# Strassen MLP behind a layer of attention on one core: copies, additions and an activation moved ahead of the fill points, two splits regrouped, the bias row by row

## The chip, the cores and the metric

The kernel runs on one NeuronCore of one Trainium2 chip. The metric is the time of one execution on the device in microseconds (us), and lower is better. A core has a matrix engine (PE, TensorE), three engines for elementwise work (DVE is VectorE, ACT is ScalarE, POOL is GpSimd), and SyncE (SP), whose queue in this kernel issues nearly all DMAs. Each engine runs its own instructions strictly in the order in which they are written; engines wait for one another only through semaphores.

## The reference, cut to what matters

The input x has 8 batches of 1024 rows of 512 values. First comes a layer of compressed attention with a residual, then an MLP with a gate and a Walsh-Hadamard transform (fwht) of its hidden values:

```
x = x + attention(layernorm(x), ...)
# attention: c = (x @ W_to_kv.T) @ W_compress.T, layernorm of c, q, k, v of width 64,
# rotary embedding of q and k, causal softmax over 1024 keys, then
# out = z @ W_to_kv + z @ W_out_res.T + b_out_res
x = x + ffn(layernorm(x), W1, W2, W3)
# ffn: hidden = fwht(silu(x @ W1.T) * (x @ W3.T)), 2048 values a row; out = hidden @ W2.T
```

## The kernel before, in words

**Passes and steps.** The MLP is done in 8 passes of 1024 rows, one for each batch, and each pass in 16 steps h = 0 to 15. A step k = 16 s + h (s is the pass) makes one block of 128 hidden features by a Strassen scheme of 7 products, j = 0 to 6, of six matmuls of 128x512 each (lines 1115 to 1117). The products gather in banks of PSUM: ACT copies the first bank out (`copy_b`, L1545) once DVE has finished with it, then a second (`copy_p5`, L1551); DVE adds (`sum_c` L2216, `sum_e` L2220); ACT makes two silus (L1572, `silu(k, 0)` and `silu(k, 1)`), and DVE multiplies each by its partner (`hidden`, L2234). Product 2 of step k+1 writes into the bank that `copy_b` clears, and `copy_b` of step k+1 waits for the last `hidden` of step k.

**The second Strassen.** Every two steps give a pair p of hidden blocks. Out of a pair seven forms are made (A11, S2, S3, A22, A12, S1, S4): sums on POOL (`form_sum`, L2554), and each form is split into a high and a low half-precision part: the high one on ACT (`parts_high`, L1593), the low one, which subtracts the high one, on DVE (`parts_low`, L2240) or on POOL (L2559). `SPLITS` says which forms are split by one instruction. Every four steps give the operands of 14 **units** of 2x6 matmuls of 128x256 (`unit`, lines 1199 to 1201), and one half of a unit follows each of the 7 products of a step. Of the units' results ACT copies some out (`take`, L1601), which POOL then adds to rows of the output (`row_add`, L2572), and DVE adds others itself (`add_unit`, L2249). From step 20 on PE thus alternates: a product, a half unit, a product, a half unit.

**The attention in between.** The attention of the next batch is done in two halves of 512 rows (a is the number of the half), and is spread over the **fill points** of the steps: after product j of step h is fill point f = 7h + j, and in each engine's program `fill(k, j)` issues what is due there. An even a has its slot 0 at f = 3, the odd a behind it 42 points later (`ODD`). The four tiles t of 128 query rows of an a start at the slots `tile_slot(a, t)`: 19, 25, 31 and 37 for an even a, 19, 27, 35 and 43 for an odd one. Names used below: `cproj` (L867, latent projection), `Kl` (L1878), `norm1` (L1928, writes V), `rope_k`/`rope_q` (L1380, L1395), `exps` (L1403 and L1408; it loads the table of the exponential), `low` (L1987, writes Pl, the low part of the softmax), `bias` (L2502, POOL, adds the output's bias to a tile's row of `ring`, four to an a), `tokens_sum`, `tokens_high`, `tokens_low` (L2208, L1538, L2198: the normalized rows for the next pass, by Strassen's forms) and `halves_sum` (L2576, L2259: halves of the rows and weights for W2's forms, made once in passes 0 and 1).

**SP's queue.** `load_forms` (L665) fetches the weights of a step's products (WS), `load_form` (L737) transposes the normalized rows into XF by DMA, `load_form2` (L703) brings W2's forms. `FORMS_AT` says at which j of a step `load_forms` stands.

**What sets the order.** The programs of the engines are written out by hand. Each engine's step function lists its own work between `fill` calls; `take_at(k, j)` and `add_at(k, j)` look up whether a unit's copy or addition is due there. Counters of semaphores (`high_no`, `low_no`) follow that order.

Of the kernel before, what the change touches and what calls it, by code (L numbers as in the profile page):

```python
# [83 lines left out]
TPREP = ({33: 0, 42: 1, 51: 2, 60: 3}, {8: 4, 22: 5, 36: 6, 50: 7})  # L84
# [9 lines left out]
FORMS_AT = {0: 2, 6: 2}  # L94
# [152 lines left out]
def build_kernel(nc, x, xT, w13, w13t, w2, small, cst, tab, wscr, w2scr, w2tmp, w2f, out):  # L247
    with ExitStack() as ctx:
# [335 lines left out]
        def _(sp):  # L584
# [91 lines left out]
            def load_halves(x):  # L676
# [3 lines left out]
                if x in (0, 4):  # L680
                    w.wait_ge(v_xf, xf_no(x // 4, 6))
# [172 lines left out]
        def _(pe):  # L854
# [485 lines left out]
        def _(ac):  # L1340
# [429 lines left out]
            for k in range(NK):  # L1770
# [12 lines left out]
                take_at(k, 0)  # L1783
# [27 lines left out]
                take_at(k, 4)  # L1811
                fill(k, 4)
# [25 lines left out]
        def _(ve):  # L1838
# [186 lines left out]
            def xnorm(a, t):  # L2025
# [3 lines left out]
                if a in (2, 4):  # L2029
                    w.wait_ge(d_tst, 32 * a)  # L2030
# [669 lines left out]
```

## Time and profile before

| | |
|---|---|
| time, median of 3 runs | 2144.19 us (2143.27 to 2144.85) |
| the profiled execution's own time | 2144.14 us |
| its span in the profile | 2142.1 us |
| PE busy | 2010.1 us, 94% |
| DVE, ACT, POOL busy | 1525.1, 1157.8, 1066.0 us |
| granted clock of PE, tenths of full speed, 40 slices | 8 in the first, 9 in the others (9 is 90% or more) |

The profile shows one execution. A row of a timeline gives start, duration, engine, line, operation, tiles, and in brackets how long the engine sat idle before it and what released it. PE's records overlap: a matmul of 128x512 is on record for 0.38 us, but the next one starts 0.22 us behind it. So when a product has to wait, PE loses the idle time in brackets and the overlap of about 0.16 us beside it.

### The profile page before, as it was taken

What the parts mean: (1) busy time and instruction counts of PE and PEld (TensorE: products, weight loads), DVE (VectorE), ACT (ScalarE), POOL (GpSimd) and SP (SyncE); (2) the same over time, 40 slices, a digit from 0 to 9 for tenths busy, and PEclk for the clock granted to TensorE, in tenths of its full rate; (3) what the DMA queues carried; (4) which work ended last, traced back from release to release, by engine and by line L of the source; (5) the groups of instructions that cost most, each with busy time, mean ns of one, the idle gap of its engine ahead of it and who ended that gap; (6) DMA issues with size and microseconds to landing.
All of it is one profiled execution on the core that took longest, in us unless ns stands there. A gap on an engine that the chain in (4) does not pass through costs nothing.

```text
span 2142.1 us, 32782 instructions
## 1 busy us (share of the span) xinstructions
PE 2010.1 (94%) x11862; PEld 1167.0 (54%) x11862; DVE 1525.1 (71%) x2626; ACT 1157.8 (54%) x1775; POOL 1066.0 (50%) x788
## 2 busy tenths in 40 slices
PE   6889899989999999999999999999999999999998
PEld 3534344455555656556555555556565555556665
DVE  7897978758777686776777677776768768653333
ACT  5866455455554655555555646556564555543343
POOL 2356732556356454554546544554644545454444
PEclk8999999999999999999999999999999999999999
DMA  8656346454463524735346434545347353373322
GB/s 328 222 193 228 123 143 164 153 156 138 121 155 125 188 88 142 173 108 164 115 116 171 148 123 123 138 138 163 113 126 178 100 163 113 100 168 125 119 96 89
DMA packets 267264, 312.57 MB, mean 146 GB/s; under 512 B 181344, under 2 KB 191712, under 8 KB 265312
## 3 DMA queue, kind: packets, MB, share of 16 engines
q1 hardware_dynamic: 267104, 310.48, 47.7%
q8 instruction: 95, 1.56, 0.3%
q14 instruction: 65, 0.53, 0.1%
HBM read 221.02 MB, written 47.19 MB: 125 GB/s over the span
## 4 chain that ended last, share of the span: by engine, by line
PE 52%; DVE 19%; ACT 10%; issue 9%; POOL 6%; DMA 3%; SPq 1%; ACTq 0%; DVEq 0%; POOLq 0%
PE PF L1115 10%; PE PF L1117 10%; PE PF L1116 10%; PE PD L1199 4%; PE PD L1200 4%; PE PD L1201 4%; DVE H L2240 2%; POOL ring L2502 2%; DVE XS L2208 2%; DMA WS<-wscr 1%; DVE W2S L2234 1%; DVE Pl L1987 1%; ACT H L1593 1%; PE XY L936 1%; ACT W2S L1572 1%
## 5 line engine op out<-in xcount | busy, mean ns | idle before, releaser
L1115 PE MATMUL PF<-XF,WS 128*128 128x512 f16 x1778 | 676.2, 380 | 25.8 <-ACT PF L1545 10.3
L1116 PE MATMUL PF<-XF,WS 128*128 128x512 f16 x1778 | 674.3, 379 | 0.0
L1117 PE MATMUL PF<-XF,WS 128*128 128x512 f16 x1778 | 674.1, 379 | 0.0
L1199 PE MATMUL PD<-W2S,H 128*128 128x256 f16 x1456 | 397.2, 273 | 33.5 <-ACT W2S L1601 14.8
L1201 PE MATMUL PD<-W2S,H 128*128 128x256 f16 x1456 | 397.1, 273 | 0.0
L1200 PE MATMUL PD<-W2S,H 128*128 128x256 f16 x1456 | 397.1, 273 | 0.0
L2572 POOL TENSOR_TENSOR ring<-ring,W2S 128x512 f32<-128x512 f32 x192 | 257.0, 1341 | 203.2 <-ACT W2S L1601 203.2
L1117 PEld LDWEIGHTS PF<-XF,WS 128*128 128x128 f16 x1778 | 174.0, 98 | 210.1 <-issue 0.7
L1115 PEld LDWEIGHTS PF<-XF,WS 128*128 128x128 f16 x1778 | 173.8, 98 | 193.0 <-issue 36.1
L2554 POOL TENSOR_TENSOR SH<-SH 128x512 f32<-128x512 f32 x112 | 162.2, 1448 | 196.0 <-DVE SH L2234 191.6
L1116 PEld LDWEIGHTS PF<-XF,WS 128*128 128x128 f16 x1778 | 174.3, 98 | 124.2 <-issue 4.8
L1545 ACT ACTIVATE PF<-PF 128x512 f32<-128x512 f32 x127 | 73.9, 582 | 291.2 <-DVE W2S L2234 136.6
L2216 DVE TENSOR_TENSOR PF<-PF,p 128x512 f32<-128x512 f32 x127 | 88.4, 696 | 183.6 <-PE PF L1117 183.6
L1199 PEld LDWEIGHTS PD<-W2S,H 128*128 128x128 f16 x1456 | 142.4, 98 | 132.5 <-issue 30.2
L1572 ACT ACTIVATE SH<-PF,afs 128x512 f32<-128x512 f32 x144 | 98.9, 687 | 206.4 <-PE PF L1117 113.2
L1200 PEld LDWEIGHTS PD<-W2S,H 128*128 128x128 f16 x1456 | 142.5, 98 | 81.3
L2554 POOL TENSOR_TENSOR W2S<-W2S,SH 128x512 f32<-128x512 f32 x56 | 75.2, 1343 | 214.7 <-DVE H L2240 214.7
L1601 ACT ACTIVATE W2S<-PD,afs 128x512 f32<-128x512 f32 x224 | 152.6, 681 | 9.8 <-PE PD L1201 8.5
L1201 PEld LDWEIGHTS PD<-W2S,H 128*128 128x128 f16 x1456 | 142.5, 98 | 16.6
L2234 DVE SCALAR_TENSOR_TENSOR SH<-PF,afs,SH 128x512 f32<-128x512 f32 x144 | 107.4, 747 | 57.8 <-ACT SH L1572 48.6
L1572 ACT ACTIVATE W2S<-PF,afs 128x512 f32<-128x512 f32 x112 | 77.0, 688 | 118.3 <-PE PF L1117 117.9
L2220 DVE TENSOR_TENSOR PF<-PF,p 128x512 f32<-128x512 f32 x127 | 87.7, 691 | 69.7 <-PE PF L1117 69.3
(371 smaller groups left out, 3606.0 us busy)
## 6 DMA issues: line engine op xcount, KB each, us to landing
WS<-wscr SPq DMA_DIRECT2D x112, 896.0 KB, 4.9
W2S<-w2f SPq DMA_DIRECT2D x196, 256.0 KB, 2.7
ring<-x SPq DMA_DIRECT2D x56, 256.0 KB, 5.3
wscr<-WS SPq DMA_DIRECT2D x16, 896.0 KB, 4.2
out<-ring SPq DMA_DIRECT2D x56, 256.0 KB, 3.2
RAW<-w13t SPq DMA_DIRECT2D x16, 512.0 KB, 4.6
xraw<-xT SPq DMA_DIRECT2D x28, 256.0 KB, 4.1
XF<-w SPq DMA_DIRECT2D x13, 512.0 KB, 18.1
```

What stands on the lines that cost most here:

```text
L1115: pe.matmul(bank, wh, th, start=i < 2 and j == 0, stop=False, skip_group_check=True)
L1116: pe.matmul(bank, wh, tl, start=False, stop=False, skip_group_check=True)
L1117: m = pe.matmul(bank, wl, th, start=False, stop=j == 1, skip_group_check=True)
L1199: pe.matmul(o, th, wh, start=i in (P1, P2, P5) and tp == 0 and r == 0, stop=False, skip_group_check=True)
L1200: pe.matmul(o, th, wl, start=False, stop=False, skip_group_check=True)
L1201: m = pe.matmul(o, tl, wh, start=False, stop=r == 1, skip_group_check=True)
L1572: ac.activation(sh(k)[:, i, :], PF[:, (1 - k % 2, 2)[i], :], ACT.Silu, scale=afs[:, k % NH:k % NH + 1]).then_inc((a_sb, a_sc2)[i], 1)
L1601: ac.activation(TT[:, u % 2, :], PD[:, u % 2, :], ACT.Copy, scale=afs[:, 65:66]).then_inc(a_T, 1)
L2216: ve.tensor_tensor(PF[:, 2, :], PF[:, k % 2, :], p5[:, :], ALU.add).then_inc(v_c, 1)
L2234: ve.scalar_tensor_tensor(o, PF[:, (k % 2, 3)[i], :], afs[:, 16 + h:17 + h], o, ALU.mult, ALU.mult).then_inc((v_hA, v_hE)[i], 1)
L2554: gp.tensor_tensor(o, a, b, op).then_inc(g_S, 1)
L2572: gp.tensor_tensor(r, r, TT[:, g, :].rearrange("p (t c) -> p t c", t=2), ALU.add).then_inc(g_r, 1)
```

## The change

- **Splits regrouped.** A12 is split by itself as soon as it is there (ACT behind `copy_b`, DVE ahead of `sum_c`); so S4 can be summed on POOL at j = 2 instead of j = 3, and S4 and A22 are split together by one instruction of 1024 columns: ACT at the end of the even step, POOL at j = 0 of the odd step. Before, A12 and A22 were one split of 1024 columns on ACT and DVE, and S4 one of 512 on ACT and POOL.
- **Copies and additions of units** stand ahead of the fill point at which they stood behind it (`take_at`, `add_at`), and `silu(k, 1)` of steps above 16 stands ahead of fill point 4. DVE's `hidden(k, 1)` stands behind fill point 5 where that one holds a `low`.
- **Bias row by row.** POOL's four additions of an attention's bias were two calls of two rows at slots 12 and 13; now each row has its own call, four slots behind its tile's start.
- **W2's halves** (`TPREP`) are prepared later: two in pass 0 and six in pass 1, where there were four and four.
- **Smaller ones.** At h = 0 `load_forms` stands at j = 1 instead of 2 on SP; `cproj` of k 0 and 1 at slot 3 instead of 2 for a from 3 on; the drain at the end is reordered.

```diff
-PLACE_A = {"A11": (0, 0), "S3": (1, 8), "S1": (2, 3), "S2": (4, 4), "A12": (5, 6), "A22": (7, 7), "S4": (16, 17)}
-SPLITS = (("A11", "S3"), ("S1", "S2"), ("A12", "A22"), ("S4",))
+PLACE_A = {"A11": (0, 0), "S3": (1, 8), "S1": (2, 3), "S2": (4, 4), "A12": (16, 17), "A22": (7, 7), "S4": (5, 6)}
+SPLITS = (("A11", "S3"), ("S1", "S2"), ("A12",), ("S4", "A22"))
-TPREP = ({33: 0, 42: 1, 51: 2, 60: 3}, {8: 4, 22: 5, 36: 6, 50: 7})
+TPREP = ({48: 0, 59: 1}, {8: 2, 18: 3, 28: 4, 38: 5, 48: 6, 58: 7})
-FORMS_AT = {0: 2, 6: 2}
+FORMS_AT = {0: 1, 6: 2}
+def low_at(k, j):
+    s, h = divmod(k, NH)
+    return s > 0 and any(slot == tile_slot(c, t) + 2 for c, slot in slots(s, 7 * h + j) for t in range(4))
 # PE
-                if slot in (2, 5):
-                    for k in (0, 1) if slot == 2 else (2, 3):
+                if slot in (2 if a < PLAIN else 3, 5):
+                    for k in (2, 3) if slot == 5 else (0, 1):
 # ACT, one step
+                if k > 4 * QF + 1 and k % 2 == 0:
+                    parts_high(k // 2 - 1, 2)
-                take_at(k, 0)
+                take_at(k, 1)
                 fill(k, 0)
                 if k:
                     copy_p5(k)
-                if k > 4 * QF + 2 and k % 2:
-                    parts_high((k - 3) // 2, 3)
-                take_at(k, 1)
+                take_at(k, 2)
                 fill(k, 1)
...
-                take_at(k, 4)
-                fill(k, 4)
+                take_at(k, 5)
+                if k <= 4 * QF:
+                    fill(k, 4)
                 silu(k, 1)
-                take_at(k, 5)
+                if k > 4 * QF:
+                    fill(k, 4)
+                take_at(k, 6)
                 fill(k, 5)
+                if k > 4 * QF + 1 and k % 2 == 0:
+                    parts_high(k // 2 - 1, 3)
-                take_at(k, 6)
 # DVE, one step
                     hidden(k - 1, 0)
+                    add_at(k, 0)
                     fill(k - 1, 6)
...
+                if k > 4 * QF + 1 and k % 2 == 0:
+                    parts_low(k // 2 - 1, 2)
-                add_at(k, 1)
+                add_at(k, 2)
                 fill(k, 1)
                     sum_c(k)
...
-                add_at(k, 5)
+                if low_at(k, 5):
+                    fill(k, 5)
                 hidden(k, 1)
-                fill(k, 5)
                 add_at(k, 6)
+                if not low_at(k, 5):
+                    fill(k, 5)
 # POOL
                     if j == 0:
+                        if k > 4 * QF + 2:
+                            parts_low((k - 3) // 2, 3)
                         form_sum(k // 2, 0)
-                    if j == 1 and k > 4 * QF + 2:
-                        parts_low((k - 3) // 2, 3)
-                    if j == 3:
+                    if j == 2:
                         form_sum(k // 2 - 1, 3)
-                if slot in (12, 13):
-                    w.wait_ge(v_V, one(a))
-                    bias(a, (2 * slot - 24, 2 * slot - 23))
+                for t in range(4):
+                    if slot == tile_slot(a, t) + 4:
+                        bias(a, (t,))
```

Three places in the engines' programs follow, before and after. The lines of the changed kernel are 6 or 7 higher from the fill on (1572 is 1578, 1601 is 1607, 2554 is 2561, 2502 is 2509).

The first is POOL between steps 54 and 57 of pass 3, before. L2502 is the bias, L2554 a form's sum, L2559 a low part, L2572 the addition of a unit's copy to rows:

```order
L2559 TENSOR_TENSOR H<-SH,H 128x2x512
L2572 TENSOR_TENSOR ring<-ring,W2S 128x2x256 x2
L2554 TENSOR_TENSOR SH<-W2S,SH 128x512
L2554 TENSOR_TENSOR SH<-SH 128x512
L2502 TENSOR_TENSOR ring<-ring,bb 128x512 x4
L2554 TENSOR_TENSOR W2S<-W2S,SH 128x512
L2554 TENSOR_TENSOR SH<-SH 128x512
L2559 TENSOR_TENSOR cst_s<-W2S,sc 128x512
L2572 TENSOR_TENSOR ring<-ring,W2S 128x2x256
L2559 TENSOR_TENSOR H<-SH,H 128x2x512
L2572 TENSOR_TENSOR ring<-ring,W2S 128x2x256
```

The same stretch after:

```order
L2579 TENSOR_TENSOR ring<-ring,W2S 128x2x256 x2
L2561 TENSOR_TENSOR SH<-W2S,SH 128x512
L2561 TENSOR_TENSOR SH<-SH 128x512
L2561 TENSOR_TENSOR W2S<-W2S,SH 128x512
L2566 TENSOR_TENSOR H<-W2S,H 128x2x512
L2561 TENSOR_TENSOR SH<-SH 128x512
L2579 TENSOR_TENSOR ring<-ring,W2S 128x2x256
L2566 TENSOR_TENSOR H<-SH,H 128x2x512
L2579 TENSOR_TENSOR ring<-ring,W2S 128x2x256
L2509 TENSOR_TENSOR ring<-ring,bb 128x512
L2561 TENSOR_TENSOR SH<-W2S,SH 128x512
L2561 TENSOR_TENSOR SH<-SH 128x512
L2561 TENSOR_TENSOR W2S<-W2S,SH 128x512
```

The four additions of the bias no longer stand between two sums of a step; single ones stand at other places, and the low part of 512 columns of L2559 is one of 128x2x512, ahead of the next step's sum.

The second place is ACT from the end of step 56 to the first split of step 57, before. L1572 is a silu, L1601 a unit's copy, L1380 to L1395 the rope, L1545 `copy_b`, L1593 a high part:

```order
L1572 ACTIVATE SH<-PF,afs 128x512
L1601 ACTIVATE W2S<-PD,afs 128x512
L1380 ACTIVATE Kh<-PB 64x512
L1382 ACTIVATE Kh<-Kh 64x512
L1572 ACTIVATE SH<-PF,afs 128x512
L1395 ACTIVATE Q<-PB 64x512
L1601 ACTIVATE W2S<-PD,afs 128x512
L1388 ACTIVATE Kl<-Kl 64x512
L1545 ACTIVATE PF<-PF 128x512
L1551 ACTIVATE p5<-PF 128x512
L1593 ACTIVATE H<-W2S 128x512
```

The same after:

```order
L1578 ACTIVATE SH<-PF,afs 128x512
L1607 ACTIVATE W2S<-PD,afs 128x512
L1578 ACTIVATE SH<-PF,afs 128x512
L1386 ACTIVATE Kh<-PB 64x512
L1388 ACTIVATE Kh<-Kh 64x512
L1607 ACTIVATE W2S<-PD,afs 128x512
L1401 ACTIVATE Q<-PB 64x512
L1599 ACTIVATE H<-W2S 128x2x512
L1394 ACTIVATE Kl<-Kl 64x512
L1551 ACTIVATE PF<-PF 128x512
L1607 ACTIVATE W2S<-PD,afs 128x512
```

The second silu and the copies stand ahead of the rope's instructions, and the high part of S4 with A22 (L1599, 128x2x512) stands between `rope_q` and `copy_b` of the next step.

The third is ACT around the exponentials of step 59, before (L1403 and L1408 are `exps`):

```order
L1572 ACTIVATE W2S<-PF,afs 128x512
L1601 ACTIVATE W2S<-PD,afs 128x512
L1403 ACT_TABLE_LOAD
L1403 ACTIVATE PB,st<-XY,st 128x896
L1408 ACTIVATE Ph<-PB 128x512
L1408 ACTIVATE Ph<-PB 128x384
L1572 ACT_TABLE_LOAD
L1572 ACTIVATE W2S<-PF,afs 128x512
L1545 ACTIVATE PF<-PF 128x512
```

And after:

```order
L1607 ACTIVATE W2S<-PD,afs 128x512
L1578 ACTIVATE W2S<-PF,afs 128x512 x2
L1409 ACT_TABLE_LOAD
L1409 ACTIVATE PB,st<-XY,st 128x896
L1414 ACTIVATE Ph<-PB 128x512
L1414 ACTIVATE Ph<-PB 128x384
L1551 ACTIVATE PF<-PF 128x512
```

Both silus of step 59 now stand ahead of the table load and the exponentials; they stood on both sides of them. On DVE, `low` of the same step now stands ahead of `hidden(59, 1)`, and stood behind it.

## Rows read from the trace of the kernel before

**Rows 1.** The page's heading and the products' group: count, busy, mean ns, idle before.

```profile
span 2142.1 us, 32782 instructions
...
L1115 PE MATMUL PF<-XF,WS 128*128 128x512 f16 x1778 | 676.2, 380 | 25.8 <-ACT PF L1545 10.3
```

**Rows 2.** Windows of passes 0, 1, 3 and 7: length, busy time (instructions) by engine, clock.

```profile
108.10:370.20 262.10, 238.49 (x1108) 110.27 (x1108) 221.00 (x377) 146.67 (x217) 136.19 (x131) 0.99 0.54 171
370.20:631.60 261.40, 245.53 (x1432) 139.48 (x1431) 188.06 (x323) 137.55 (x203) 131.75 (x93) 0.99 0.50 144
...
883.70:1135.80 252.10, 241.51 (x1499) 144.56 (x1497) 186.98 (x318) 140.05 (x210) 128.42 (x89) 1.00 0.47 137
...
1892.10:2142.10 250.00, 237.90 (x1514) 147.29 (x1511) 97.81 (x118) 95.27 (x141) 123.45 (x92) 1.00 0.36 114
```

**Rows 3.** Waits of PE in pass 3 (883.7 to 1135.8): total us, times, longest.

```profile
PE PD L1199 <- ACT W2S L1601: 3.2, 3, 1.4
...
PE PF L1115 <- DVE SH L2234: 0.9, 2, 0.5
PE XY L867 <- DVE Kl L1878: 0.8, 1, 0.8
PE PD L1199 <- DVE WX L2249: 0.8, 1, 0.8
PE XY L922 <- DVE Q L1966: 0.5, 1, 0.5
...
PE PF L1115 <- DMA WS<-wscr: 0.4, 1, 0.4
```

**Rows 4.** Timeline of POOL, step 57: the bias and the sum behind it.

```profile
1016.39 6.94 POOL L2502 TENSOR_TENSOR ring<-ring,bb 128x512 f32<-128x512 f32 x4 [4.19 <-DVE V L1928]
...
1024.97 1.26 POOL L2554 TENSOR_TENSOR W2S<-W2S,SH 128x512 f32<-128x512 f32 x1
```

**Rows 5.** Timeline of ACT there: second silu, rope of the queries.

```profile
1026.32 0.69 ACT L1572 ACTIVATE SH<-PF,afs 128x512 f32<-128x512 f32 x1 [1.12 <-POOL W2S L2554]
1029.27 0.63 ACT L1395 ACTIVATE Q<-PB 64x512 fp32r<-64x512 f32 x1 [2.26 <-DVE PB L1954]
```

**Rows 6.** Timeline of PE in step 57: two half units that waited.

```profile
1030.75 0.27 PE L1199 MATMUL PD<-W2S,H 128*128 128x256 f16 x1 [1.43 <-ACT W2S L1601]
...
1040.21 0.27 PE L1199 MATMUL PD<-W2S,H 128*128 128x256 f16 x1 [0.65 <-ACT W2S L1601]
```

**Rows 7.** Timeline of ACT at the start of step 51: `copy_b`.

```profile
937.01 0.58 ACT L1545 ACTIVATE PF<-PF 128x512 f32<-128x512 f32 x1 [0.22 <-DVE SH L2234]
```

**Rows 8.** Timelines in steps 59 and 60: table load and `copy_b` on ACT, `low` on DVE.

```profile
1068.01 1.28 ACT L1403 ACT_TABLE_LOAD   x1
...
1077.97 0.58 ACT L1545 ACTIVATE PF<-PF 128x512 f32<-128x512 f32 x1 [3.96 <-DVE W2S L2234]
...
1074.72 2.22 DVE L1987 SCALAR_TENSOR_TENSOR Pl<-PB,Ph 128x512 f16<-128x512 f32 x2
```

**Rows 9.** Last pass: PE's wait for XF, and the landing of XF's transposes.

```profile
1905.51 0.39 PE L1115 MATMUL PF<-XF,WS 128*128 128x512 f16 x1 [0.89 <-DMA XF<-Pl]
...
DMA to landing us min/median/max: 3.1/3.1/3.2
```

**Rows 10.** Timelines of DVE and POOL in step 48: one operation of DVE twice.

```profile
888.01 1.21 DVE L2198 TENSOR_TENSOR PB<-XS,PB 128x1024 f16<-128x1024 f32 x1
...
891.68 2.29 DVE L2198 TENSOR_TENSOR Pl<-XS,Ph 128x1024 f16<-128x1024 f32 x1
...
891.16 1.73 POOL L2572 TENSOR_TENSOR WX<-WX,W2S 128x512 f32<-128x512 f32 x1 [3.25 <-ACT W2S L1601]
```

**Rows 11.** POOL's low parts by form in pass 3: 1024 and 512 columns.

```profile
L2559 POOL TENSOR_TENSOR H<-SH,H 128x1024 f16<-128x1024 f32 x8 | 17.0, 2128 | 0.0
...
L2559 POOL TENSOR_TENSOR H<-W2S,H 128x512 f16<-128x512 f32 x4 | 4.6, 1160 | 6.6 <-ACT H L1593 6.6
```

**Rows 12.** Timeline of PE in pass 0: the longest wait there.

```profile
244.96 0.40 PE L892 MATMUL XY<-id,V 128*128 128x128 f16 x4 [2.90 <-DVE V L1928]
```

More of the change, by code:

```diff
@@ L75 @@
 HFORM = ("A11", "S2", "S3", "A22", "A12", "S1", "S4")
-PLACE_A = {"A11": (0, 0), "S3": (1, 8), "S1": (2, 3), "S2": (4, 4), "A12": (5, 6), "A22": (7, 7), "S4": (16, 17)}
-PLACE_B = {"A11": 9, "S3": 10, "S1": 11, "S2": 12, "A12": 13, "A22": 14, "S4": 15}
-SPLITS = (("A11", "S3"), ("S1", "S2"), ("A12", "A22"), ("S4",))
+PLACE_A = {"A11": (0, 0), "S3": (1, 8), "S1": (2, 3), "S2": (4, 4), "A12": (16, 17), "A22": (7, 7), "S4": (5, 6)}
+PLACE_B = {"A11": 9, "S3": 10, "S1": 11, "S2": 12, "A12": 15, "A22": 14, "S4": 13}
+SPLITS = (("A11", "S3"), ("S1", "S2"), ("A12",), ("S4", "A22"))
 SPLIT_OF = {f: i for i, fs in enumerate(SPLITS) for f in fs}
 WFILE = (4, 0, 1, 2, 5, 3, 6)
-TPREP = ({33: 0, 42: 1, 51: 2, 60: 3}, {8: 4, 22: 5, 36: 6, 50: 7})
+TPREP = ({48: 0, 59: 1}, {8: 2, 18: 3, 28: 4, 38: 5, 48: 6, 58: 7})
 SPLIT_AT = {13 + i: i for i in range(16)}
@@ L200, in high_no @@
 def high_no(p, i):
-    return 16 + 4 * (p - 2 * QF) + i + 1
+    return 16 + 4 * (p - 2 * QF) + {0: 1, 2: 2, 1: 3, 3: 4}[i]
 def low_no(p, i):
-    return 2 * (p - 2 * QF) + {0: 1, 3: 2, 1: 17, 2: 18}[i]
+    return 2 * (p - 2 * QF) + {0: 1, 3: 2, 2: 17, 1: 18}[i]
 def sum_no(p, i):
@@ L502, in parts_from @@
         def parts_from(p, i):
-            return (SH[:, :, :], SH[:, :, :], SHO[:, :, :], SHO[:, 0, :])[i]
+            return (SH[:, :, :], SH[:, :, :], SHO[:, 0, :], SHO[:, :, :])[i]
         def parts_free(p, i):
@@ L679, in load_halves @@
                 w.wait_ge(d_w2st[q % 2], 224)
-                if x in (0, 4):
-                    w.wait_ge(v_xf, xf_no(x // 4, 6))
+                if x in (0, 2):
+                    w.wait_ge(v_xf, xf_no(x // 2, 6))
                 else:
@@ L1796, in _ @@
                     parts_high(k // 2, 0)
-                take_at(k, 2)
-                if k > 4 * QF + 1 and k % 2 == 0:
-                    parts_high(k // 2 - 1, 2)
                 if split and k > 1:
@@ L1802, in _ @@
                     forms_high(h + 1, 1)
+                take_at(k, 3)
                 fill(k, 2)
@@ L1805, in _ @@
                     silu(k, 0)
-                take_at(k, 3)
+                take_at(k, 4)
                 fill(k, 3)
@@ L1823, in _ @@
                     norms(14, 0)
-                take_at(k, 6)
                 if k % 4 < 3:
                     fill(k, 6)
+            parts_high(NK // 2 - 1, 2)
             parts_high(NK // 2 - 1, 1)
             take(NK // 4 - 1, 0)
-            parts_high(NK // 2 - 1, 2)
             take(NK // 4 - 1, 1)
-            take(NK // 4 - 1, 2)
             parts_high(NK // 2 - 1, 3)
-            for u in COPIED[3:]:
+            for u in COPIED[2:]:
                 take(NK // 4 - 1, u)
@@ L2029, in xnorm @@
                 if a in (2, 4):
-                    w.wait_ge(d_tst, 32 * a)
+                    w.wait_ge(d_tst, 16 * (2, 8)[a // 2 - 1])
                 ve.tensor_scalar(XS[:, a % 2, t, :], xrow(a, t), st[:, 184 + 2 * t:185 + 2 * t], st[:, 84 + t:85 + t],
@@ L2238, in parts_low @@
                 w.wait_ge(a_hi, high_no(p, i))
-                w.wait_ge(g_S, sum_no(p, 2))
                 ve.tensor_tensor(parts_at(p, i, 1), parts_from(p, i), parts_at(p, i, 0), ALU.subtract).then_inc(v_lo, 1)
@@ L2451, in _ @@
                     tokens_sum(0, 6)
-                add_at(k, 0)
                 fill(k, 0)
@@ L2462, in _ @@
                     parts_low(k // 2 - 1, 1)
-                add_at(k, 2)
                 fill(k, 2)
-                if k > 4 * QF + 1 and k % 2 == 0:
-                    parts_low(k // 2 - 1, 2)
                 if k and s == 0 and h < NH - 1:
                     forms_low(h + 1, 0)
-                add_at(k, 3)
+                add_at(k, 4)
                 fill(k, 3)
@@ L2476, in _ @@
                     forms_low(h + 1, 1)
-                add_at(k, 4)
+                add_at(k, 5)
                 fill(k, 4)
                 out_rows(k // 4 - 1, 2 * (k % 4))
-                add_at(k, 5)
+                if low_at(k, 5):
+                    fill(k, 5)
                 hidden(k, 1)
-                fill(k, 5)
                 add_at(k, 6)
+                if not low_at(k, 5):
+                    fill(k, 5)
                 if k == 0:
@@ L2487, in _ @@
             add_at(NK, 0)
+            parts_low(NK // 2 - 1, 2)
             parts_low(NK // 2 - 1, 1)
-            parts_low(NK // 2 - 1, 2)
             for u in ADDED:
```

## The prediction

> **What bounds the kernel now.** I read the page first: its heading gives the span, 2142.1 us [rows 1]. The execution's own time is 2144.14 us, so 2.0 us lie outside the span, and it stands 0.05 us under the median of the runs shown. My sum is made against 2144.14 and taken for the median as it is.
>
> The reader is to see next in the table of windows [rows 2] that PE is busy nearly all the time at full clock: 241.51 of 252.10 us in pass 3. Passes 2 to 6 are alike to 0.1 us, so an edit that saves 1 us in one of them saves 5. Passes 0 and 1 take 262.10 and 261.40 us, the last 250.00. The work of PE isn't changed; only its waits can go. A matmul of 128x512 is on record for 380 ns [rows 1], and the next starts some 0.22 us behind its start, so a wait in brackets costs its idle time plus about 0.16 us. By that measure a pass has some 14 us of waits that have a name, of 252.
>
> Third, the waits of PE in pass 3 [rows 3] say who is late: ACT's copies of units three times (3.2 us), DVE's `hidden` twice (0.9), `Kl` and the addition to WX (0.8 each), Q (0.5), one DMA of weights (0.4). None is long, and none of these engines is full (DVE 187 of 252 us, ACT 140, POOL 128 [rows 2]). So it is order inside the queues that bounds PE, and for that I read the timelines of the engines around each wait and moved the rows into the new order.
>
> **The change part by part**, first for a pass of the middle, as us gained or lost.
>
> *Bias row by row, copies earlier (step 57): +2.75.* POOL's four additions take 6.94 us from 1016.39 on, and waited 4.19 us for V [rows 4]. Behind them is the sum that the second silu needs: it starts at 1024.97 and ends at 1026.2. The silu follows at 1026.32, `rope_q` at 1029.27 [rows 5], the unit's copy right behind that, and PE's half unit starts at 1030.75 after 1.43 us idle [rows 6]: 1.6 us with the overlap. A second one at 1040.21 costs 0.65, or 0.8. The silu's lateness also makes `hidden` late, half of the 0.9 us of [rows 3], with the overlap 0.56. Together 2.97 us. In the new order a single addition (1.74 us, a quarter of 6.94) stands there, and the copy is ahead of `rope_q`. I leave 0.2 us of waiting: +2.75.
>
> *The same in step 50: +1.85.* Three waits in 4 us of time: `hidden` 0.5, the addition to WX 0.8, Q 0.5 [rows 3], with overlap 2.3 us. The silu and the addition go ahead of the rope; the POOL block is gone. `copy_b` of step 51 had 0.22 us idle before it [rows 7], and now has the high part of S4 and A22 ahead of it: I leave 0.45 us.
>
> *Steps 48 and 49: -0.7 and +0.4.* With `load_forms` one product earlier the wait for WS (0.4) goes, and with `cproj` one slot later the wait for `Kl` (0.8, with overlap 0.95) goes too. But product 6 of step 48 then comes to its XF earlier, and XF is just in time. The last pass, which has no `cproj`, shows it: PE idle 0.89 us for XF, whose transposes land 3.1 us behind their issue [rows 9]. The same product would wait 1.2 to 2.1 us here, as the loading of WS now lies beside these transposes: between -0.3 and -1.15, taken as -0.7.
>
> *Step 59: -0.6.* Silu 1 moves ahead of `exps`, whose table load takes 1.28 us from 1068.01 [rows 8]. It has to wait for product 5, which ends at about 1071.4, so table, exponentials and `Ph` end 1 us or so later than now; DVE then does `low` (2.22 us for two) ahead of the last `hidden`, and `copy_b`, now at 1077.97, comes 0.6 us later. Product 2 of step 60 waits for it. Ends: 0 if DVE's order makes up for it, -1.3 if the table load is moved whole.
>
> *Other places, +0.75:* step 52, where silu and copy come earlier, +0.65; step 63, the third copy of 3.2 us, delayed by the normalized rows' work, +0.5; steps 61 and 62, where `sum_c` comes later behind the split of A12, -0.2 each. I bound these together by 0 and +1.5.
>
> *The regrouped splits.* ACT has the same work. DVE does 512 columns where it did 1024: eight times in a pass some 0.5 us less. POOL does 1024 where it did 512, 2.128 against 1.160 us [rows 11], so 8 times 0.97 us more. POOL is busy half the time and PE waits for it nowhere in [rows 3], so this costs nothing by itself; its cover is the step between the form's sum and its unit.
>
> *DVE beside POOL: -0.5.* One operation, the low part of the tokens, takes DVE 1.21 us at 888.01 and 2.29 us at 891.68, with POOL's addition of 1.73 us beside it from 891.16 [rows 10]. The new POOL split lies at j = 0 of odd steps, where DVE mostly multiplies from PSUM or adds units; only a few of its instructions there read two operands from SBUF. The most it could cost is the time that is new on POOL, 7.8 us a pass (eight times 0.97), if all of it were on the path; the least nothing. I take one hit of 1.1 us in two passes, 0.5 a pass, as DVE has 65 of 252 us idle.
> The Trainium skill ("SBUF — State Buffer", section "Who interferes with whom") says that a VectorE instruction with both inputs in SBUF and a GpSimd instruction that reads SBUF shut one another out for the whole instruction. The doubled row agrees. With every new split on the path by that rule, a middle pass would lose 3.4 us instead of gaining 3.95; this case stands with the slower rival.
>
> The sum for a middle pass: 2.75 + 1.85 - 0.7 + 0.4 - 0.6 + 0.75 - 0.5 = 3.95 us, and 19.75 for five.
>
> *Pass 1: +1.* It has the terms of steps 57, 59 and 60 (+2.75, -0.6, +0.5 less the port's 0.5) and no units before step 20, so no gain of step 50. Two more preparations of halves fall into it, each some 4.9 us of POOL: about -1.2. *Pass 0: +2.* It loses two of them. Its longest wait is 2.90 us for V [rows 12], behind a `halves_sum` on DVE and a chain of small ones beside POOL; half of it and a little more should go. Ends -1 and +6. *Last pass: +0.5*: the wait for WS there goes, the one for XF of 0.89 us doubles.
>
> All: 19.75 + 1 + 2 + 0.5 = 23.25. 2144.14 - 23.25 = 2120.9, so 2121 us.
>
> **The rivals.**
>
> *The gain is mostly taken over by the next late instruction.* Where one wait goes, PE comes earlier to the next one, whose chain hangs on DVE or a DMA and not on PE. For it: DVE is the busiest helper (187 of 252 us), the rope's chain for Q and the step around V are DVE alone, and POOL's low part of 2.128 us [rows 11] may double DVE's rows. Against: DVE's waits in [rows 3] sum to 3.0 us, ACT's to 3.2. Then only the bias's two unit waits (2.4 us) are kept and 1.2 us lost elsewhere: 1.2 a pass, 6 in five, 1 in the others: 2137 us, somewhere from 2130 to 2140.
>
> *Nothing moves*, because W2's halves in pass 1 and the later `exps` eat what is left of that: within 4 us of 2144.
>
> *Slower: the high part of S4 and A22 is in the way of `copy_b`.* It takes ACT about 1.05 us, waits for POOL's sum of S4, and is directly ahead of `copy_b` of all eight odd steps. Where `copy_b` is late, product 2 waits for it and all behind. It decides when ACT has less than 1.05 us idle ahead of `copy_b`. For it: 0.22 us at step 51 [rows 7]. Against: 3.96 us at step 60 [rows 8], and S4's sum comes a product earlier than before. If it bites by 0.8 us in all eight odd steps of 6.5 passes, 42 us are lost and 23 gained: 2163 us. If in a few, 2150. POOL's new 7.8 us a pass, all on the path of DVE, would end at the like: 2121 plus 7.3 in five passes, 2158; it is 0.03 of this rival's chance.
>
> **How the numbers follow.** Two executions of this kernel differ by up to 1.6 us; I call 0.2%, 4.3 us, no change. Chances: the forecast 0.60, its own range 2109 to 2130; the takeover 0.20, of which a fifth ends within 0.2%; nothing moves 0.08; the slower one 0.12. The range starts at 2107, where each cost is at its better end (5.5 us in each middle pass, 3 in pass 1, 6 in pass 0), and reaches to 2143, through the takeover into "nothing moves". Faster by over 0.2% is the forecast and most of the takeover, 0.76; within 0.2% 0.12; slower 0.12.
>
> **What would show it.** Right: no wait of PE over 0.3 us for ACT's unit copies in step 57; POOL's L2509 in single rows of 1.3 to 1.8 us; passes 2 to 6 of 248 us; a wait for XF in product 6 of step 48 and one for `copy_b` of about 1.7 us in step 60. The bias step is wrong if the two half units of step 57 still wait, the step on splits if `copy_b` in odd steps becomes a regular wait. I am wrong as a whole if the middle passes aren't under 251 us.

## The result: 2166.38 us, slower by 1%, and the profile after

The changed kernel takes 2166.38 us (median of 4 runs, 2164.94 to 2167.83) against 2144.24 for the one before: a ratio of 1.0104, 95% interval 1.0086 to 1.0121. That is 22 us slower where 23 us faster was forecast, and outside the range.

The page of the changed kernel has the span (its execution took 2164.94 us) and the products' group, which answer to [rows 1]:

```profile
span 2163.1 us, 32679 instructions
...
L1121 PE MATMUL PF<-XF,WS 128*128 128x512 f16 x1778 | 677.8, 381 | 62.0 <-DVE PF L2223 17.2
```

Idle time ahead of products grew from 25.8 to 62.0 us; ahead of half units (L1205, on the same page) it fell from 33.5 to 9.6. The windows of passes 0, 1, 3 and 7, cut at the changed kernel's own pass starts, answer to [rows 2] (length, then busy time and count by engine, granted clock):

```profile
107.40:361.80 254.40, 236.01 (x1108) 109.75 (x1108) 214.25 (x375) 144.57 (x215) 122.00 (x123) 1.00 0.53 168
361.80:634.80 273.00, 247.94 (x1432) 139.65 (x1431) 191.57 (x325) 139.89 (x205) 150.56 (x101) 0.99 0.49 146
889.80:1146.40 256.60, 243.25 (x1499) 145.13 (x1498) 183.44 (x318) 139.95 (x210) 130.94 (x89) 0.99 0.48 135
1912.90:2163.10 250.20, 238.11 (x1514) 147.18 (x1512) 92.17 (x118) 98.17 (x141) 130.54 (x92) 1.00 0.37 114
```

Pass 0 gained 7.7 us (262.1 to 254.4), pass 1 lost 11.6 (261.4 to 273.0), each middle pass lost 3 to 4.5 (252.1 to 255.0 up to 256.6), the last nothing. The waits of PE in pass 3 (total us, times, longest) answer to [rows 3]:

```profile
PE PF L1121 <- DVE PF L2223: 2.6, 2, 1.3
PE XY L887 <- ACT PB L1363: 2.5, 2, 1.3
PE PF L1121 <- DMA XF<-Pl: 2.0, 1, 2.0
PE PF L1121 <- DVE W2S L2241: 1.4, 1, 1.4
PE PF L1121 <- DVE PF L2227: 1.2, 1, 1.2
PE PF L1121 <- ACT PF L1551: 1.1, 1, 1.1
```

The waits for unit copies (3.2 us) are gone, as forecast. In their place stand waits that were not there: for `sum_c` (L2223), for the copy of the latent projection (L1363), for XF, for the last `hidden` (L2241), for `sum_e` (L2227).

The longest wait of PE inside the passes is in pass 1, step 22 (longer ones stand only ahead of pass 0 and in the drain at the end, in both kernels). PE's row at its end and the clock of the stretches behind it (the third number from the end is the granted clock):

```profile
480.06 0.77 PE L952 MATMUL XY<-Mh,oh 128*128 128x512 f32 x1 [4.40 <-issue]
```

```profile
475.00:480.00 5.00, 0.67 (x7) 0.35 (x4) 2.37 (x4) 3.26 (x5) 3.81 (x3) 0.85 0.07 24
480.00:483.00 3.00, 2.94 (x7) 1.29 (x8) 1.30 (x2) 0.48 (x1) 0.00 (x0) 0.50 0.00 0
483.00:486.00 3.00, 3.00 (x13) 1.52 (x12) 0.89 (x2) 1.21 (x2) 0.00 (x0) 0.61 0.00 0
486.00:489.00 3.00, 3.00 (x18) 1.86 (x17) 2.97 (x5) 1.20 (x2) 0.00 (x0) 1.00 0.86 257
```

A wait of 4.4 us, and behind it six microseconds at the lower of PE's two levels or mixed. Ahead of it POOL is busy from 464.79 to 470.5 with a preparation of halves (5.5 us), then adds a unit's copy; the forms' sums come behind that, and ACT's high part waits for them:

```profile
475.37 1.06 ACT L1599 ACTIVATE H<-SH 128x1024 f16<-128x1024 f32 x1 [3.27 <-POOL SH L2561]
```

DVE's low part waits for ACT's (2.98 us), and behind that low part, on DVE and then on ACT, stands the `ol` that PE's next instruction needs.

### The profile page after: what moved, and what is told of

Same layout as the page of the kernel before. It is cut to its first block, busy times and chain, and to the rows that moved or that the text cites. A ratio compares the mean times of both kernels' runs of the same rounds, so it can differ in the third digit from the quotient of the medians.

```text
span 2163.1 us, 32679 instructions
## 1 busy us (share of the span) xinstructions
PE 2011.6 (93%) x11862; PEld 1166.7 (54%) x11862; DVE 1498.3 (69%) x2626; ACT 1162.6 (54%) x1775; POOL 1089.8 (50%) x788
## 4 chain that ended last, share of the span: by engine, by line
PE 52%; DVE 22%; issue 10%; ACT 9%; POOL 3%; DMA 2%; SPq 1%; ACTq 0%; DVEq 0%; POOLq 0%
PE PF L1121 10%; PE PF L1123 10%; PE PF L1122 10%; PE PD L1205 4%; PE PD L1207 4%; PE PD L1206 4%; DVE XS L2215 2%; DVE W2S L2241 2%; ACT L1409 2%; DVE ring L2255 1%; DVE XS L2038 1%; DMA XF<-Pl 1%; ACT PB L1409 1%; PE XY L942 1%; POOL ring L2579 1%
## 5 line engine op out<-in xcount | busy, mean ns | idle before, releaser
L1205 PE MATMUL PD<-W2S,H 128*128 128x256 f16 x1456 | 397.8, 273 | 9.6 <-POOL H L2566 4.4
L2566 POOL TENSOR_TENSOR H<-W2S,H 128x1024 f16<-128x1024 f32 x56 | 121.9, 2178 | 302.7 <-ACT H L1599 302.7
L1205 PEld LDWEIGHTS PD<-W2S,H 128*128 128x128 f16 x1456 | 142.5, 98 | 101.5 <-DVE H L2246 7.7
L2223 DVE TENSOR_TENSOR PF<-PF,p 128x512 f32<-128x512 f32 x127 | 88.4, 696 | 103.4 <-PE PF L1123 103.4
L2561 POOL TENSOR_TENSOR SH<-W2S,SH 128x512 f32<-128x512 f32 x56 | 73.5, 1313 | 152.0 <-DVE W2S L2241 151.9
L1599 ACT ACTIVATE H<-SH 128x1024 f16<-128x1024 f32 x112 | 117.9, 1053 | 42.0 <-POOL SH L2561 42.0
```

The lines of the kernel that those rows point to most:

```text
L1205: pe.matmul(o, th, wh, start=i in (P1, P2, P5) and tp == 0 and r == 0, stop=False, skip_group_check=True)
L1599: ac.activation(parts_at(p, i, 0), parts_from(p, i), ACT.Copy).then_inc(a_hi, 1)
L2561: gp.tensor_tensor(o, a, b, op).then_inc(g_S, 1)
L2566: gp.tensor_tensor(parts_at(p, i, 1), parts_from(p, i), parts_at(p, i, 0), ALU.subtract).then_inc(g_lo, 1)
```

## The experiments

The change has seven separable parts: the bias row by row, the regrouped splits, the unit copies (ACT), the second silu (ACT), DVE's additions with `hidden(k, 1)`, the two loads at h = 0 (`load_forms`, `cproj`), and W2's halves. Seven runs take parts out of the changed kernel, the others add them to the kernel before. Lengths of passes, and waits with the overlap of 0.16 us counted in, are read from each run's trace; figures taken from the brackets of a row are without it. A ratio's interval of 0.15% either way is 3 us, so a difference of two runs under some 4 us is not told from none. The drain's new order has no run of its own.

### Parts taken out of the changed kernel

**The silu put back.**

```diff
-                if k <= 4 * QF:
-                    fill(k, 4)
+                fill(k, 4)
                 silu(k, 1)
-                if k > 4 * QF:
-                    fill(k, 4)
```

> The changed kernel with one thing put back: ACT's fill point 4 stands ahead of the second silu again. Theory A (the moved silu is what costs): the copy of the latent projection (L1363) stands in fill point 4, and behind the silu it waits for product 5, so PE waits 1.43 us for it twice in a pass (12 times in all), and 0.77 us for ol once; these go, with the longer wait for copy_b in step 60 in part: 3.6 to 4.3 us a pass, 22 to 26 in all, 2141 to 2145 us. Rival B (the waits only change their name, since rope_q and the copy of a unit come late again): under 1 us a pass is gained, 2160 to 2166 us.

Measured 2154.56 us, ratio 1.0043 (1.0028 to 1.0057): 12 us gained, between the two expectations. Theory A's main term fell: L1363's waits of 1.43 us stayed, so they are not the silu's. In pass 3 the wait of step 60 (1.60) went, and the one for `copy_b` in step 48 (1.29).

**The splits put back** (both engines' `parts_high` and `parts_low`, `form_sum` 3 at j = 3).

> The changed kernel with the splits put back: A12 with A22 in one split on ACT and DVE, S4 by itself, the sum of S4 at j = 3. Theory A (the moved silu costs): the waits for sum_c in steps 62 and 63 (1.5 us each) get shorter, unit waits of 1.1 and 1.3 come back, 2162 to 2169 us. Rival C (the splits cost, by POOL's 1024 columns beside DVE and by the part ahead of sum_c): 3 us a pass, and most of step 22's 4.6 us, are gained, 2140 to 2150 us.

Measured 2161.75 us, 1.0076 (1.0061 to 1.0091): 5 us gained, with intervals that touch. That is just under Theory A's figure, and a misleading one, as the runs below show.

**The additions put back**, with `hidden(k, 1)` ahead of fill point 5.

> The changed kernel with DVE's additions of units behind their fill points again and hidden(k, 1) ahead of fill point 5. Theory A: the wait for sum_c in step 62 (1.5) shrinks by the addition's 0.74, the wait for sum_e in step 57 (1.41) stays, since a low part of the softmax is ahead of it, unit waits of 1.1 come back: 2162 to 2168 us. Rival D (the additions ahead of sum_c and sum_e are what costs): 2.5 us a pass are gained, 2148 to 2153 us.

Measured 2153.47 us, 1.0040 (1.0027 to 1.0053): 13 us gained, near rival D; its six runs spread over 8 us.

**W2's halves put back.**

> The changed kernel with W2's halves prepared at the old places, four in pass 0 and four in pass 1. Theory: pass 0 loses again the 7.7 us that it gained, pass 1 gets back the 7.7 us of step 22 (a wait of 4.6 us and matmuls at a lower clock behind it) and 1 to 3 more: 2162 to 2166 us, about no change. Rival (step 22's wait comes from the bias and the splits, not from the halves): step 22 keeps its wait, 2172 to 2175 us.

Measured 2167.32 us, 1.0104 (1.0089 to 1.0120): no change. Pass 0 loses 6.8 us again, pass 1 gains 5.1; step 22's wait is gone. So that wait hangs on the halves' 5.5 us on POOL ahead of step 22.

**The copies put back**: each `take_at` behind its fill point.

> The changed kernel with ACT's copies of units (take) behind their fill points again. Theory T: in steps 49 and 55 the copy of a unit now stands ahead of the copy of the latent projection (L1363) and waits for the half unit on PE that used to hide that copy; PE then waits 1.43 us, 12 times in all. With the copies put back these go, 17 us, and the wait for Kl in step 51 (0.68) too, while unit waits as in step 57 before (1.6) may come back in part: 2145 to 2150 us. Rival (the silu or DVE's additions set these waits): L1363's waits stay, 2160 to 2168 us.

Measured 2185.38 us, 1.0193 (1.0178 to 1.0208): 19 us *slower*. Theory T fell in this form. L1363's wait went down from 1.43 to 0.17 in step 55, but rose to 1.73 in step 49, and half units waited again, 2.75 us in step 57 alone. Something else was late on ACT.

**The loads put back** (`FORMS_AT` 2, slot 2).

> The changed kernel with the weights' load of h = 0 at j = 2 and cproj at slot 2 as before. Theory: the wait for XF of 2.2 us in each of seven first steps goes, with the lower clock that came with it in pass 3 (1.5 us); the waits for Kl (0.95) and WS (0.5; 1.6 in the last pass) come back: 4 to 7 us gained, 2159 to 2163 us. Rival (XF is late by the change of DVE's and ACT's order, not by these two edits): XF's wait stays beside the others, 2168 to 2174 us.

Measured 2171.71 us, 1.0128 (1.0113 to 1.0143): 5 us slower. Neither expectation: XF's wait is gone, as the theory had it, but `Kl`'s and the weights' cost more than it did. In pass 3 they are 0.66 and 0.65 us for `Kl` and 0.70 for WS, with 1.09 for XL in step 54, which the kernel before did not have there.

**All three moves put back.**

> The changed kernel with all three moves ahead of the fill points put back (copies, additions with hidden(k, 1), silu); splits, bias row by row, W2's halves and the loads as changed. Theory: the three moves are what made the kernel slower: L1363's 17 us go, and 15 to 20 us of the waits for copy_b, hidden and sum_c that the moves of the silu and the additions made; some unit waits come back: 2132 to 2142 us. Rival (the regrouped splits and the halves in pass 1 cost as much): 2145 to 2155 us.

Measured 2181.03 us, 1.0175 (1.0158 to 1.0192), slower than the changed kernel. Both expectations fell: what is left of the change, the splits, the loads and the halves beside the bias, is 37 us slower than the kernel before. Taking parts out did not sum up, so I turned the question round.

### The bias alone, and parts added to it

**The kernel before with the bias row by row.**

```diff
-                if slot in (12, 13):
-                    w.wait_ge(v_V, one(a))
-                    bias(a, (2 * slot - 24, 2 * slot - 23))
+                for t in range(4):
+                    if slot == tile_slot(a, t) + 4:
+                        bias(a, (t,))
```

The run has two more edits, small ones, which all the kernels built on it share: in every fourth step unit 0's copy stands behind the high part of A12 with A22 on ACT, not ahead of it, and the drain has the changed kernel's order of copies. No run separates them from the bias.

> The kernel before with the bias row by row alone. Theory: POOL's block of 6.9 us ahead of the form's sum in step 57 goes, with it both unit waits there (1.6 and 0.8) and the wait for hidden (0.56), and in step 51 most of 2.3 us: 3 to 4.5 us in each of five middle passes and 2.5 in pass 1, 2121 to 2128 us. Rival (the waits pass to Q and V, whose chain is DVE's): 1 us a pass, 2138 to 2143 us.

Measured 2124.58 us, 0.9909 (0.9894 to 0.9923): 20 us faster. Pass 3 takes 248.2 us. Its POOL timeline at the place of [rows 4] has no bias and starts the sum at 1016.66, 2.4 us idle before it; counted from the start of the pass that is 7.2 us earlier than before:

```profile
1016.66 1.26 POOL L2557 TENSOR_TENSOR W2S<-W2S,SH 128x512 f32<-128x512 f32 x1 [2.36 <-DVE H L2245]
1017.88 1.27 POOL L2575 TENSOR_TENSOR ring<-ring,W2S 128x512 f32<-128x512 f32 x1
```

**Splits beside the bias, and the same with one order changed.** The second kernel differs from the first in this alone:

```diff
                     if j == 0:
-                        if k > 4 * QF + 2:
-                            parts_low((k - 3) // 2, 3)
                         form_sum(k // 2, 0)
+                        if k > 4 * QF + 2:
+                            parts_low((k - 3) // 2, 3)
```

> The kernel before with two parts of the change: bias row by row, and the regrouped splits. Theory S (the splits are the loss: POOL's low part of 1024 columns stands ahead of the sum for A11 and S3 at j = 0 of odd steps, ACT's next high part waits for that sum, and exponentials, latent copy and silu are queued behind it): 5 to 7 us a pass more than with the bias alone, and step 22's 4.6 us, 2160 to 2172 us. Rival (the loads and the halves are the loss): 2124 to 2132 us.

> As the run with bias and splits, with one order changed on POOL: at j = 0 of odd steps the sum for A11 and S3 stands ahead of the low part of S4 and A22, not behind it. Theory S by the order: ACT's high part no longer waits 2.3 us for the sum, and most of the loss is gone, 2124 to 2140 us. Rival (it is the 1024 columns on POOL beside DVE, or the part of A12 ahead of sum_c): within 4 us of the run with bias and splits.

Measured 2158.60 us, 1.0066 (1.0051 to 1.0081), and with the order changed 2137.68 us, 0.9970 (0.9957 to 0.9982). The first is just under Theory S's range, the second within its own. So the splits cost 34 us beside the bias (0.0157 of 2144), and 21 of them are the order of two instructions on POOL. Step 57 of pass 3 shows how. POOL and ACT with the low part first:

```profile
1033.91 2.14 POOL L2561 TENSOR_TENSOR H<-W2S,H 128x1024 f16<-128x1024 f32 x1
1035.99 1.28 POOL L2556 TENSOR_TENSOR SH<-SH 128x512 f32<-128x512 f32 x1
```

```profile
1037.31 1.06 ACT L1599 ACTIVATE H<-SH 128x1024 f16<-128x1024 f32 x1 [2.34 <-POOL SH L2556]
1038.38 1.28 ACT L1409 ACT_TABLE_LOAD   x1
...
1043.32 0.68 ACT L1607 ACTIVATE W2S<-PD,afs 128x512 f32<-128x512 f32 x1
```

```profile
1044.15 0.27 PE L1205 MATMUL PD<-W2S,H 128*128 128x256 f16 x1 [2.59 <-ACT W2S L1607]
```

With the sum first (its POOL, ACT and PE):

```profile
1031.23 1.27 POOL L2556 TENSOR_TENSOR SH<-SH 128x512 f32<-128x512 f32 x1
1032.46 2.13 POOL L2561 TENSOR_TENSOR H<-W2S,H 128x1024 f16<-128x1024 f32 x1
```

```profile
1032.54 1.06 ACT L1599 ACTIVATE H<-SH 128x1024 f16<-128x1024 f32 x1 [0.25 <-POOL SH L2556]
```

```profile
1039.38 0.27 PE L1205 MATMUL PD<-W2S,H 128*128 128x256 f16 x1 [0.49 <-ACT W2S L1607]
```

POOL itself is never what PE waits for here. ACT waits 2.34 instead of 0.25 us for the sum; the exponentials, a silu and a unit's copy are queued behind that wait, and PE waits for the copy: 2.59 us instead of 0.49. In passes 3 and 5 the lower clock follows this wait, and they are 1.1 to 1.7 us longer than passes 2, 4 and 6. Of the 13 us that remain with the order changed, three waits of pass 3 are the largest: WS in step 49 (1.26 us), `Kl` in step 51 (1.14, where it was 0.47 for Q; the high part of 1024 columns stands ahead of the keys' low part on ACT), and `hidden` and ol in step 58 (0.47 and 1.20, where it was 0.69).

**The three moves beside the bias.**

> The kernel before with the bias row by row and the three moves ahead of the fill points (copies, additions with hidden(k, 1), silu). Theory: the copies cost the latent copy's 1.43 us twice a pass, the silu and the additions gain and lose alike: 2.5 to 4 us a pass more than with the bias alone, 2138 to 2148 us. Rival (the moves help here as they did beside the splits, by 15 us): 2108 to 2118 us.

Measured 2159.60 us, 1.0074 (1.0059 to 1.0089): 35 us more than the bias alone, more than either expectation.

**The loads beside the bias.**

> The kernel before with the bias row by row, cproj at slot 3 and the weights' load of h = 0 at j = 1. Theory: the waits for Kl (0.95) and WS (0.5) in the first two steps go and one for XF of 1.8 to 2.4 us comes: 0.4 to 2.5 us a pass more than with the bias alone, 2127 to 2138 us. Rival (XF's transposes land in time once POOL and DVE have their old order): 1.5 us a pass are gained, 2115 us.

Measured 2136.56 us, 0.9963 (0.9950 to 0.9976): 12 us more, in the theory's range. In pass 3 this wait stands where the bias alone has 0.77 us for `Kl` (PE):

```profile
901.12 0.39 PE L1121 MATMUL PF<-XF,WS 128*128 128x512 f16 x1 [2.01 <-DMA XF<-Pl]
```

Its cause stands on SP's queue. With the bias alone the load of WS is issued behind the last transpose, here it is ahead of the last two, and the issue of the last takes 3.24 us instead of 1.23 (in the other middle passes 3.19 to 3.74). With the bias alone, then with the loads moved:

```profile
891.86 1.23 SPq L743 DMA_TRANSPOSE XF<-Pl  x1
893.14 0.58 SPq L671 DMA_DIRECT2D WS<-wscr  x1
```

```profile
893.42 0.58 SPq L671 DMA_DIRECT2D WS<-wscr  x1
894.04 1.24 SPq L743 DMA_TRANSPOSE XF<-Ph  x1
895.82 3.24 SPq L743 DMA_TRANSPOSE XF<-Pl  x1
```

In the changed kernel XF has a second cause: in pass 3 that issue takes only 1.70 us, but starts at 901.46, when DVE has made the rows' low part, 1.8 us later than in these two runs, counted from `sum_c` of step 48. DVE had waited 1.18 us for ACT's high part, and its own low part ahead took 1.92 us instead of 1.23.

**Each move by itself beside the bias, and the halves.** The edits are those of the change, one at a time.

> The kernel before with the bias row by row and ACT's unit copies alone ahead of the fill points. Theory T (the copies are the largest part of the 35 us of the three moves): the latent copy waits behind them, 1.43 us twice a pass, 17 us in all, less the unit waits of 0.4 to 1.3 us in steps 57 and 63: 2130 to 2142 us. Rival (silu or additions carry it): 2115 to 2126 us.

> The kernel before with the bias row by row and the second silu alone ahead of fill point 4. Theory T: the exponentials come 1 us later in some steps, PE waits for PT or ol or copy_b there: 0 to 2 us a pass more than the bias alone, 2124 to 2136 us. Rival (the silu carries the 35 us): 2145 to 2160 us.

> The kernel before with the bias row by row and, on DVE alone, the additions ahead of the fill points and hidden(k, 1) behind fill point 5 where a low part is due. Theory T: ring waits (1.1, 0.4) go, the wait of step 60 grows from 0.85 to 1.6: within 6 us of the bias alone, 2119 to 2131 us. Rival (the additions carry the 35 us, by sum_c and V coming later): 2145 to 2160 us.

> The kernel before with the bias row by row and W2's halves at the new places (two in pass 0, six in pass 1). Theory: pass 0 gains 7 us as it did in the whole change, pass 1 loses 3 to 8 in steps 20 to 24, where POOL's 4.9 us of halves stand among the units' additions: 2120 to 2126 us. Rival (pass 1 loses as much as in the whole change, 11 us or more): 2128 to 2136 us.

Copies 2138.48 us, 0.9967 (0.9953 to 0.9981); silu 2146.75, 1.0008 (0.9998 to 1.0017); additions 2124.68, 0.9906 (0.9892 to 0.9921); halves 2125.35, 0.9907 (0.9893 to 0.9922). Against the bias alone: about 12, 21, 0 and 0 us. Copies, additions and halves came as their theories said; for the silu the theory fell and the rival's figure came. The three moves (copies, silu, additions) add up to 33 us, near the 35 us measured with all three in one kernel. The first two, on ACT and then PE, in step 49 for the copies and in step 48 for the silu:

```profile
910.82 0.69 ACT L1607 ACTIVATE W2S<-PD,afs 128x512 f32<-128x512 f32 x1 [1.49 <-PE PD L1207]
911.41 0.59 ACT L1363 ACTIVATE PB<-XY 128x512 f32<-128x512 f32 x1
```

```profile
912.05 0.66 PE L887 MATMUL XY<-cst_s,PB 128*128 128x128 f32 x4 [1.27 <-ACT PB L1363]
```

```profile
898.22 0.69 ACT L1578 ACTIVATE SH<-PF,afs 128x512 f32<-128x512 f32 x1 [3.24 <-POOL W2S L2560]
898.81 0.62 ACT L1353 ACTIVATE Kh<-xraw 128x512 fp32r<-128x512 f32 x1
```

```profile
900.21 0.80 PE L873 MATMUL XY<-Kh,Wc 128*128 128x512 f32 x1 [2.25 <-DVE Kl L1886]
```

Without the move, in the kernel before, the latent copy is done in time and PE does not wait (ACT, then PE):

```profile
906.50 0.60 ACT L1357 ACTIVATE PB<-XY 128x512 f32<-128x512 f32 x1
```

```profile
907.31 0.60 PE L881 MATMUL XY<-cst_s,PB 128*128 128x128 f32 x4
```

Both are one pattern. The copy waits 1.49 us for the half unit on PE; the latent copy used to run *in the shadow* of that half unit, and now stands behind it, so PE ends the half unit and finds nothing to do. The silu waits 3.24 us for POOL's sum, and with it the conversion of the keys, which needs nothing of it: without the move that conversion stands ahead of the silu (it ran at 892.50, the silu at 895.88), and PE waited 0.77 us. That wait is 1.5 us of the 3.1 us that a middle pass loses; 1.06 for XL in step 54, 0.53 for ol in step 53 and 0.8 more for `copy_b` in step 60 come with it, some small waits go, and in three passes the clock falls (last section). The halves move some 7 us from pass 0 to pass 1. The additions are neutral, but `hidden(k, 1)` behind the low part cuts step 60's wait (0.85) to nothing over 0.15.

### A version that beats both

Bias, `hidden(k, 1)` behind fill point 5 where that holds a low part, halves spread anew (r1); and that with the copies moved only at h = 14 and 15, the silu only at h = 3 and 9 (r2).

```diff
+TPREP = ({39: 0, 49: 1, 59: 2}, {8: 3, 16: 4, 24: 5, 36: 6, 50: 7})
+                if low_at(k, 5):
+                    fill(k, 5)
                 hidden(k, 1)
 # r2, on ACT
+                early = h in (14, 15)
+                take_at(k, 0 + early)
+                if s > 0 and h in (3, 9):
+                    fill(k, 4)
```

> The kernel before with the bias row by row, hidden(k, 1) behind fill point 5 where that holds a low part, and W2's halves at fill points 39, 49, 59 of pass 0 and 8, 16, 24, 36, 50 of pass 1. Theory: against the bias alone 0.85 us less in step 60 and its like of six passes, and 3 to 6 us less in pass 0: 2114 to 2121 us. Rival (both are taken over by later waits, in steps 10 to 12 and 20 to 25): 2122 to 2127 us.

> As run r1, with ACT's unit copies ahead of the fill points in steps h = 14 and 15 alone, and the second silu ahead of fill point 4 in steps h = 3 and 9 alone. Theory: 0.3, 0.4, 0.4 and 0.4 us a pass less: 4 to 9 us under r1. Rival (each is followed by a wait of the same size in the next step): within 2 us of r1.

Measured 2121.22 us, 0.9884 (0.9867 to 0.9900), and 2120.70 us, 0.9883 (0.9868 to 0.9898): 24 us faster than the kernel before, and alike; against the bias alone that is 3 to 4 us, with intervals that touch. The middle passes of both are 0.9 us shorter than with the bias alone, all of it from step 60. Step 63's wait fell by 0.44 us in r2, and step 48's wait for `copy_b` rose by 0.45: the rival of r2.

## Why the prediction was wrong

- **Bias row by row: right.** The term (2.75, and part of 1.85 at step 50) measured by itself (with the two small edits named above) 19.8 us, 3.9 in pass 3. The three waits of step 57 in [rows 3 to 6] fell from 2.97 to 1.17 us, not to the 0.2 I left.
- **"POOL is busy half the time and PE waits for it nowhere in [rows 3], so this costs nothing by itself": the step that failed most.** The splits cost 34 us beside the bias (taken out of the whole change they gave back 5). PE's waits name only the last link, and the prediction's own bias term, [rows 4 to 6], was such a chain, from POOL over ACT to PE. I moved every instruction to its new place, but priced the wider one at its own engine and not at ACT, which waits for the sum behind it with everything in its queue. That this order costs 21 us is shown beside the bias; no run changes it within the whole change. The rival with ACT's high part ahead of `copy_b` had the right size and the wrong place: the waits for `copy_b` in odd steps stayed under 0.25 us but in pass 1.
- **Copies and silu earlier, counted as gains at steps 50, 52, 57 and 63 and -0.6 at step 59: wrong sign.** Beside the bias 12 and 21 us are lost. Within the whole change the silu loses 12 us too, but there the copies gain 19. At the places I looked at, the unit waits did go; I didn't ask at each fill point that was passed what stood in it. The latent copy and the conversions stand there, and PE needs them.
- **Steps 48 and 49, -0.7 and +0.4: under-sized.** The wait for XF was 2.2 us in pass 3, just over the far end of what I gave (2.1); beside the bias the two edits lose 12 us, not 2. The loading of WS, which I had beside the transposes, is ahead of the last two on their queue and lengthens the last one's issue; a lower clock follows the wait in some passes (last section).
- **Passes 0 and 1, +2 and +1: measured +7.7 and -11.6.** With the halves 7 us move from pass 0 to pass 1, sum zero. I had the direction of the halves, not the sign of pass 1, and missed step 22, where 5.5 us of POOL among the units led to a wait of 4.4 us. The last pass, +0.5, measured -0.2.
- **Step 60** got its wait of about 1.6 us, as said, though the profile names `hidden` (L2241) for it and not `copy_b`.
- **DVE beside POOL, -0.5: real, its size open.** The tokens' low part doubled beside the wide split in step 63 of the changed kernel (DVE, then POOL):

```profile
1132.82 2.48 DVE L2205 TENSOR_TENSOR PT<-XS,PT 128x1024 f16<-128x1024 f32 x1
```

```profile
1131.90 2.33 POOL L2566 TENSOR_TENSOR H<-W2S,H 128x1024 f16<-128x1024 f32 x1 [7.43 <-ACT H L1599]
```

  By the Trainium skill ("SBUF — State Buffer", section "Who interferes with whom") a VectorE instruction with two SBUF inputs contends with a GpSimd instruction that reads SBUF. This row agrees: 2.48 us, where the same operation took 1.21 in [rows 10]. How much of the splits' other 13 us is this remains open; no run separates it from the split of A12 ahead of `sum_c`.
- **The sum itself.** Parts beside the bias add to -20 + 34 + 12 + 21 - 1 + 12 - 0 = 58 us; measured are 22. They hide one another: with the splits and the rest in, the copies' move gains 19 us, beside the bias alone it loses 12. The three moves together cost 35 us beside the bias, but beside bias, splits, loads and halves they gain 15 (2181.03 to 2166.38); by which waits the two groups hide one another, no run shows. No sum of single terms could have given the time.

## What to carry to other kernels

When an instruction is moved ahead of another on an in-order engine, price what it *waits for* and charge that to everything that it now stands in front of, the unrelated work first; a copy that waits for PE must not stand ahead of work that was hidden behind that same PE work. An engine that PE never waits for can still set the time through a second engine's queue. When a change has several parts, build up from the kernel before: here taking parts out one by one would have kept the bad ones and hidden that one part alone was worth 20 us.

## What the runs showed of the hardware that was not expected

Behind a wait of some 2 us or more the granted clock of PE sometimes fell to the lower level of 1.2 GHz, and sometimes not, at the same place of the same program. The changed kernel waits for XF at the start of each middle pass. In pass 2 the clock behind that wait (2.35 us with the overlap) stays at 1.00, in pass 3 (2.21) it reads 0.54 and 0.60 for four microseconds:

```profile
650.00:652.00 2.00, 1.75 (x11) 1.00 (x12) 0.36 (x1) 0.00 (x0) 0.82 (x1) 1.00 1.04 344
652.00:654.00 2.00, 2.00 (x12) 1.17 (x10) 0.41 (x1) 1.07 (x2) 0.00 (x0) 1.00 0.93 303
```

```profile
905.00:907.00 2.00, 1.83 (x5) 0.73 (x6) 0.43 (x1) 0.00 (x0) 0.89 (x1) 0.54 0.91 283
907.00:909.00 2.00, 2.00 (x10) 1.18 (x9) 0.00 (x0) 0.00 (x0) 0.00 (x0) 0.60 0.99 313
```

It costs 1.5 us there. In r1 and r2, alike in pass 0, PE waits 2.81 and 2.89 us for `ol` at about 211.6; from 211 to 217 the clock is 0.72 in the one and 1.00 in the other, and r1 lost 3.4 us more than r2 in that pass, through this and two later places. The clearest case is the run with the silu alone beside the bias. PE waits the same 2.25 us for `Kl` at the start of each middle pass; behind it the clock fell in passes 3, 5 and 6 and not in 2 and 4, and these passes took 252.8, 253.0 and 253.3 us against 251.3 and 251.4: in this execution some 5 of the silu's 21 us are clock. The four microseconds behind the wait in passes 2 and 5:

```profile
649.00:653.00 4.00, 4.00 (x23) 2.23 (x24) 3.38 (x4) 0.92 (x3) 2.41 (x2) 1.00 0.99 333
1404.50:1408.50 4.00, 4.00 (x14) 1.92 (x15) 3.02 (x4) 0.85 (x2) 1.34 (x2) 0.59 0.83 281
```

So two kernels' single profiles may differ by microseconds that neither edit made, and a wait near 2 us costs more on average than its length.
